# A two-layer LoRA kernel in fp32: W's fourth pair loaded earlier, the images stored by GpSimd, and sums of W's blocks kept one group sooner for two of five products

## The chip, the cores and the metric

One Trainium2 chip, one core. The metric is the device time of the kernel in microseconds, the median of several executions; lower is better.

## What is computed

```python
x = x + (x @ B[id0].T) @ A[id0].T              # layer 0, adapter of rank 16, scaling 1
x = x + x @ W.T + b + 2 * ((x @ A1[id1].T) @ B1[id1])   # layer 1, adapter of rank 16, scaling 2
```

x is 8 x 512 x 2048, W is 2048 x 2048, everything is float32, and each of the 8 batch elements ("units") has its own adapters. Nearly all arithmetic is x @ W.T.

## The kernel before

**The multiplication.** Each number is split into a high part in fp32r and a low part, and a product is made of three matmuls: high by high, low by high, high by low (L530, L531, L532). Two units of x make a group, so there are four groups. Within a group a Strassen-like scheme of seven products over half matrices replaces eight. Five of the seven products (i = 0, 1, 2, 4, 6) need a sum or a difference of two blocks of W; products 3 and 5 need one block only. A product has eight steps (o = 0 to 7), one for each 128 rows of output, so there are 4 x 7 x 8 = 224 steps, numbered s. A step is 24 matmuls of 128 x 512.

**W.** For step s SyncE loads a block into `w_one` (three slots) and, where a sum is wanted, a second block into `w_two` (two slots), `load_w`. VectorE adds the pair in place (L672, `sum_w`), ScalarE makes the high part (L567) and VectorE the low part (L676, `split_w`). In group 0 all sums are made and thrown away; in group 1 they are made again and stored to `w_sums` in device memory (`keep_sum`); groups 2 and 3 load the stored sums. A `w_one` slot whose sum is stored is reloaded only after that store has landed.

**The adapters.** Work in the background is cut into chunks, and `background(s)` says which chunks go between the matmuls of step s: the first after c = 1 of the step's eight columns c, the second after c = 5, the third after c = 6. In group 0, steps 3 to 16, the 32 chunks are rows of W multiplied with layer 0's A (six matmuls each, L482 to L484); they make four "images" of 128 x 512, and chunk 8j + 7 ends image j. Chunks from step 19 on multiply x with the down adapters (four matmuls, L500 and L501). A chunk's raw data comes by SyncE (`bg_raw`, three slots at first), ScalarE makes its high part (L597), VectorE its low part (L703); there are two buffers for the parts, so that the split of chunk z waits until TensorE is through chunk z - 2. Before step 3 TensorE makes `across` from all units' a1 and a0 (L551).

**Images.** TensorE ends image j with a matmul that needs `b1_rows`; VectorE adds it to the `image` tile, where eight rows of a0 per j have been loaded (L804, one step after the image's last chunk and behind the splits for the step after that). SyncE stores the tile to `images` (L406), two steps of its loop later. GpSimd's queue does the loading, in order: eight `b1_rows` transfers for image j once image j - 1 is done on TensorE, a wait for the store of image j - 1, and eight `image` transfers (L448).

**Order of the queues.** Every engine runs its own loop over s, in program order. VectorE in step s does: the adding of step s - 1's result, the low part of W for s + 1, sums and splits of x for the next product at certain o (`X_SUM_AT`, `X_SPLIT_AT`), the sum of W for s + 2, the splits of the chunks of step s + 1, the rest. At o = 7 the last two splits of x for the next product (L698) come at the very end. ScalarE has the same order. SyncE in step s does: `keep_sum(s + 1)`, `load_w(s + 3)`, loads of x, `store(s - 2)`, the raw chunks of step s + 2, the loads of `sums` for s + 2, the store of an image. Ahead of its loop it loads W for steps 0 to 2, the resident halves of x in quarters (`resident`), eight a1 adapters, the mask and the bias; only then comes W for step 3.

Of the kernel before, what the change touches and what calls it, by code (L numbers as in the profile page):

```python
# [36 lines left out]
SUMMED = [0, 1, 2, 4, 6]  # L37
STAGED = [1, 2, 3, 5, 6]
# [3 lines left out]
SUM_GROUPS = 2  # L42
# [5 lines left out]
X_SPLIT_AT = (2, 4, 7, 7)  # L48

# [15 lines left out]
def background(s):  # L65

    if s >= STEPS:
        return []
    g, i, o = where(s)
    if g:  # L70
        places = (0, 2, 4, 5)
        return [IMAGE + 16 * g + 4 * i + places.index(o)] if i < 4 and o in places else []
    if 3 <= s <= 16:
        first = 2 * (s - 3) + max(0, s - 8) // 2
        return list(range(first, first + (3 if s in (9, 11, 13, 15) else 2)))
    if 19 <= s <= 22:
        return [IMAGE + 2 * (s - 19), IMAGE + 2 * (s - 19) + 1]
    return [IMAGE + 8 + s - 24] if 24 <= s <= 31 else []
# [39 lines left out]
def has_sum(s):  # L118

    return 0 <= s < SUM_GROUPS * PER_GROUP and where(s)[1] in SUMMED  # L120


def keeps_sum(s):
    return has_sum(s) and where(s)[0] == SUM_GROUPS - 1
# [33 lines left out]
def build(nc, x, ids0, ids1, a0, a0_down, b0, w, w_rows, bias, a1, b1, mask, w_sums, images, out):  # L158
    with ExitStack() as ctx:
# [127 lines left out]
        def _(sp):  # L287
            def load_w(s):
                g, i, o = where(s)
                one, two = W_BLOCKS[i]  # L290
                if s >= W_ONES:
                    sp.wait_ge(w_ready, s - W_ONES + 1)
                    if keeps_sum(s - W_ONES):
                        sp.wait_ge(w_kept[s % W_ONES], DMA * kept_in_slot(s - W_ONES))
                if g >= SUM_GROUPS and two:
                    made = PER_GROUP * (SUM_GROUPS - 1) + s % PER_GROUP
                    sp.wait_ge(w_kept[made % W_ONES], DMA * kept_in_slot(made))
                    source = w_sums[SUMMED.index(i), o]
                else:
                    source = w[H * one[1] + o][:, H * one[0]:H * (one[0] + 1), :]  # L300
                sp.dma_start(w_one[s % W_ONES][:, :, :], source).then_inc(w_one_loaded[s % W_ONES], DMA)
                if two and g < SUM_GROUPS:
                    k = sums_before(s)
                    if k >= W_TWOS:
                        sp.wait_ge(w_summed, k - W_TWOS + 1)
                    sp.dma_start(w_two[k % W_TWOS][:, :, :], w[H * two[1] + o][:, H * two[0]:H * (two[0] + 1), :])\
                      .then_inc(w_two_loaded[k % W_TWOS], DMA)
# [68 lines left out]
            for r in range(1, CH):  # L376
                load_resident(0, 0, r)
            sp.wait_ge(ids_loaded, 2 * DMA)
            for n in range(NB):
                sp.dma_start(a1_raw[:, n, :, :], adapter(n, a1).rearrange("u p c r -> (u p) c r"))\  # L380
                  .then_inc(a1_loaded, DMA)
            sp.dma_start(mask_sb, mask).then_inc(mask_loaded, DMA)
            sp.dma_start(bias_sb[:, :], bias).then_inc(bias_loaded, DMA)
            for s in range(STEPS):
# [3 lines left out]
                if s + W_ONES < STEPS:  # L388
                    load_w(s + W_ONES)
                if o in X_LOAD_AT and p + 1 < PRODUCTS * GROUPS:  # L390
                    load_x(p + 1, X_LOAD_AT.index(o))
# [11 lines left out]
                if s - 2 in IMAGE_LAST:  # L403
                    j = IMAGE_LAST[s - 2]
                    sp.wait_ge(image_ready, j + 1)
                    sp.dma_start(images[:, T * j:T * (j + 1)], image[:, :]).then_inc(image_stored, DMA)  # L406
# [6 lines left out]
        def _(pool):  # L413
# [24 lines left out]
            def load_rows(j):  # L438
                cols = slice(T * j, T * (j + 1))
                if j:  # L440
                    pool.wait_ge(image_done, j)
                for n in range(NB):
                    pool.dma_start(b1_rows[R * n:R * (n + 1), :], adapter(1, n, b1).rearrange("u r d -> (u r) d")[:, cols])\
                        .then_inc(b1_rows_loaded, DMA)
                if j:
                    pool.wait_ge(image_stored, DMA * j)
                for n in range(NB):
                    pool.dma_start(image[R * n:R * (n + 1), :], adapter(0, n, a0).rearrange("u r d -> (u r) d")[:, cols])\  # L448
                        .then_inc(a0_rows_loaded, DMA)

# [8 lines left out]
            for s in range(STEPS):  # L459
                g, i, o = where(s)  # L460
                if s + 4 in FIRST:
                    load_down(FIRST[s + 4])
                if i + 1 in RANKED and o == 3:
# [3 lines left out]
        def _(pe):  # L467
# [78 lines left out]
            for s in range(3):  # L546
                step(s)
# [5 lines left out]
            for s in range(3, STEPS):  # L553
# [4 lines left out]
        def _(act):  # L558
# [76 lines left out]
            for s in range(STEPS):  # L635
# [4 lines left out]
                if s == 1:  # L640
                    act.wait_ge(a0_loaded, NB * DMA)
                    act.activation(a0_hi[:, :, :, :], a0_raw[:, :, :, :].rearrange("p n c r -> p c n r"), ACT.Copy)\
                       .then_inc(a0_hi_ready, 1)
                    act.wait_ge(a1_loaded, NB * DMA)
                    act.activation(a1_cols.rearrange("p (c n r) -> p c n r", c=C, n=NB),
                                   a1_raw[:, :, :, :].rearrange("p n c r -> p c n r"), ACT.Copy).then_inc(a1_ready, 1)
                if o in X_SPLIT_AT[:2] and p + 1 < PRODUCTS * GROUPS:
                    split_x(p + 1, X_SPLIT_AT.index(o))
# [16 lines left out]
        def _(dve):  # L665
# [106 lines left out]
            for s in range(STEPS):  # L772
# [6 lines left out]
                if p + 1 < PRODUCTS * GROUPS:  # L779
                    if o in X_SUM_AT:  # L780
                        sum_x(p + 1, X_SUM_AT.index(o))
                    if o in X_SPLIT_AT[:2]:
                        split_x(p + 1, X_SPLIT_AT.index(o))
# [12 lines left out]
                if s == 3:  # L796
# [57 lines left out]
```

## Time and profile before

| | |
|---|---|
| median of 3 runs | 1407.84 us (1407.28 to 1408.16) |
| the profiled execution | 1408.91 us, its span 1407.2 us |
| TensorE busy | 98% of the span, granted clock 0.994 on the mean |
| VectorE, ScalarE, GpSimd busy | 70%, 35%, 7% |
| DMA | 329.37 MB, 234 GB/s over the span |

TensorE's matmuls start one after another without a gap for most of the span. So the time is what TensorE must do, plus the places where it waits or runs at half clock, and these lie almost all in the first 200 us and around two borders between groups.

### The profile page before, as it was taken

Reading aid. Unit: us, or ns where it says so; the run is one execution under the profiler, and the core shown is the slowest. Engines: PE = TensorE matmul, PEld = TensorE weight load, DVE = VectorE, ACT = ScalarE, POOL = GpSimd, SP = SyncE. Lnnn points to the kernel's source line nnn. Section 1 sums busy time; section 2 is a strip of 40 time slices with the busy share of each in tenths; the row PEclk is TensorE's granted clock in tenths of the full one; section 3 lists DMA queues with packets and bytes.
Section 4 is the critical chain, followed back from the end, with each engine's and each line's share of the span. In section 5 each row is a group of like instructions: output and inputs, shape, how many; then the busy total and the mean of one; then the engine's idle time right before and its main releaser. Section 6 shows DMA issues by size and latency. Waiting matters only on the chain.

```text
span 1407.2 us, 16162 instructions
## 1 busy us (share of the span) xinstructions
PE 1372.3 (98%) x5992; PEld 1127.3 (80%) x5992; DVE 983.2 (70%) x1031; ACT 485.5 (35%) x491; POOL 91.7 (7%) x190
## 2 busy tenths in 40 slices
PE   6799989999999999999999999999999999999999
PEld 5687868888887888888887888888888888888887
DVE  4888877786768887687766676666655766666662
ACT  3344334333333344233323343333233334332331
POOL 3012310001000000000001000000101000000000
PEclk9899999999999999999999999999999999999999
DMA  9888974797989888599898335556856444457642
GB/s 346 275 296 296 298 237 129 234 309 261 301 279 354 301 299 294 178 332 354 266 353 275 128 120 157 169 189 211 275 199 228 140 138 135 155 171 249 196 153 83
DMA packets 108654, 329.37 MB, mean 234 GB/s; under 512 B 14496, under 2 KB 15648, under 8 KB 108576
## 3 DMA queue, kind: packets, MB, share of 16 engines
q1 hardware_dynamic: 102240, 316.79, 67.0%
q0 software_dynamic: 6336, 11.55, 2.8%
q8 instruction: 48, 0.79, 0.2%
q14 instruction: 30, 0.25, 0.0%
HBM read 272.70 MB, written 55.57 MB: 233 GB/s over the span
## 4 chain that ended last, share of the span: by engine, by line
PE 89%; DVE 3%; DMA 3%; issue 2%; SPq 1%; ACT 1%; POOLq 0%; POOL 0%; DVEq 0%; ACTq 0%
PE acc L530 27%; PE acc L531 27%; PE acc L532 27%; PE acc L514 2%; PE down_ps L500 2%; PE down_ps L501 2%; DMA w_two<-w 1%; PE image_ps L482 1%; PE image_ps L484 1%; PE image_ps L483 1%; DVE w_one L672 1%; DMA w_sums<-w_one 1%; DVE bg_lo L703 1%; DVE w_lo L676 1%; DMA bg_raw<-x 1%
## 5 line engine op out<-in xcount | busy, mean ns | idle before, releaser
L530 PE MATMUL acc<-x_hi,w_hi 128*128 128x512 f32 x1792 | 703.6, 393 | 15.9 <-DVE x_lo L698 11.5
L531 PE MATMUL acc<-x_lo,w_hi 128*128 128x512 f32 x1792 | 700.7, 391 | 0.0
L532 PE MATMUL acc<-x_hi,w_lo 128*128 128x512 f32 x1792 | 700.3, 391 | 0.0
L567 ACT ACTIVATE w_hi<-w_one 128x1024 fp32r<-128x1024 f32 x224 | 237.5, 1060 | 673.7 <-PE acc L532 606.1
L530 PEld LDWEIGHTS acc<-x_hi,w_hi 128*128 128x128 f32 x1792 | 338.3, 189 | 88.7 <-issue 13.5
L531 PEld LDWEIGHTS acc<-x_lo,w_hi 128*128 128x128 f32 x1792 | 338.4, 189 | 71.8 <-issue 1.0
L532 PEld LDWEIGHTS acc<-x_hi,w_lo 128*128 128x128 f32 x1792 | 337.8, 188 | 71.4
L676 DVE TENSOR_TENSOR w_lo<-w_one,w_hi 128x1024 fp32r<-128x1024 f32 x224 | 273.7, 1222 | 104.9 <-ACT w_hi L567 104.9
L698 DVE TENSOR_TENSOR x_lo<-x_stage,x_hi 128x1024 fp32r<-128x1024 f32 x80 | 96.1, 1222 | 45.2 <-ACT x_hi L586 45.1
L586 ACT ACTIVATE x_hi<-x_stage 128x1024 fp32r<-128x1024 f32 x80 | 83.4, 1056 | 115.2 <-DVE x_stage L692 85.2
L741 DVE SCALAR_TENSOR_TENSOR sums<-acc,bias_sb,sums 128x512 f32<-128x512 f32 x128 | 95.7, 747 | 36.2 <-PE acc L514 36.2
L672 DVE TENSOR_TENSOR w_one<-w_one,w_two 128x1024 f32<-128x1024 f32 x80 | 97.5, 1218 | 25.8 <-DMA w_two<-w 25.8
L703 DVE TENSOR_TENSOR bg_lo<-bg_raw,bg_hi 128x1024 fp32r<-128x1024 f32 x64 | 77.5, 1220 | 27.6 <-ACT bg_hi L597 27.4
L597 ACT ACTIVATE bg_hi<-bg_raw 128x1024 fp32r<-128x1024 f32 x64 | 67.1, 1053 | 71.6 <-PE image_ps L484 49.5
L692 DVE TENSOR_TENSOR x_stage<-x_stage,resident 128x1024 f32<-128x1024 f32 x64 | 78.0, 1219 | 1.7 <-DMA x_stage<-x 1.7
L434 POOL DMA_DIRECT2D rank_raw<-images x48 | 23.4, 487 | 836.3 <-issue 836.3
L500 PE MATMUL down_ps<-bg_hi,down 128*128 128x512 f32 x128 | 51.2, 400 | 9.5 <-DVE down L747 6.0
L726 DVE TENSOR_TENSOR sums<-sums,acc 128x512 f32<-128x512 f32 x32 | 22.0, 687 | 44.7 <-PE acc L532 44.7
L514 PE MATMUL acc<-rank_x,rank_w 96*128 96x512 f32 x128 | 51.0, 399 | 0.0
L501 PE MATMUL down_ps<-bg_lo,down 128*128 128x512 f32 x128 | 50.4, 394 | 0.0
L724 DVE TENSOR_TENSOR sums<-sums,acc 128x512 f32<-128x512 f32 x32 | 21.8, 683 | 31.0 <-PE acc L532 31.0
L731 DVE TENSOR_TENSOR sums<-sums,acc 128x512 f32<-128x512 f32 x32 | 21.9, 684 | 26.5 <-PE acc L532 26.5
(53 smaller groups left out, 626.8 us busy)
## 6 DMA issues: line engine op xcount, KB each, us to landing
w_one<-w SPq DMA_DIRECT2D x144, 512.0 KB, 5.5
w_two<-w SPq DMA_DIRECT2D x80, 512.0 KB, 7.3
w_one<-w_sums SPq DMA_DIRECT2D x80, 512.0 KB, 3.3
x_stage<-x SPq DMA_DIRECT2D x64, 512.0 KB, 4.7
out<-sums SPq DMA_DIRECT2D x128, 256.0 KB, 4.5
w_sums<-w_one SPq DMA_DIRECT2D x40, 512.0 KB, 4.9
resident<-x SPq DMA_DIRECT2D x32, 512.0 KB, 7.7
sums<-x SPq DMA_DIRECT2D x64, 256.0 KB, 5.4
```

The costliest lines, as they stand in the source:

```text
L500: pe.matmul(down_ps[:, :], weights, hi[:, u, :], start=(c == 0), stop=False)
L514: pe.matmul(acc[s % BANKS][:, :], rank_w[:, P * o:P * (o + 1)], rank_x[side][:, :], start=False, stop=True, skip_group_check=True).then_in ...
L530: pe.matmul(ps[:, :], w_hi[ws][:, c, :], hi, start=(c == 0), stop=False)
L531: pe.matmul(ps[:, :], w_hi[ws][:, c, :], lo, start=False, stop=False)
L532: mm = pe.matmul(ps[:, :], w_lo[ws][:, c, :], hi, start=False, stop=(c == H - 1))
L567: act.activation(w_hi[s % W_PARTS][:, :, :], w_one[s % W_ONES][:, :, :], ACT.Copy).then_inc(w_hi_ready, 1)
L586: act.activation(x_hi[q % X_PARTS][:, :, :], x_source(p, r), ACT.Copy).then_inc(x_hi_ready, 1)
L672: dve.tensor_tensor(one, one, w_two[k % W_TWOS][:, :, :], W_SIGN[where(s)[1]]).then_inc(w_summed, 1)
L676: dve.tensor_tensor(w_lo[s % W_PARTS][:, :, :], w_one[s % W_ONES][:, :, :], f32(w_hi[s % W_PARTS][:, :, :]), ALU.subtract).then_inc(w_read ...
L698: dve.tensor_tensor(x_lo[q % X_PARTS][:, :, :], x_source(p, r), f32(x_hi[q % X_PARTS][:, :, :]), ALU.subtract).then_inc(x_ready, 1)
L703: dve.tensor_tensor(bg_lo[z % 2][:, :, :], bg_source(z), f32(bg_hi[z % 2][:, :, :]), ALU.subtract)\
L741: dve.scalar_tensor_tensor(out=tile, in0=acc[s % BANKS][:, :], scalar=bias_sb[:, f:f + 1], in1=tile, op0=ALU.add, op1=ALU.add).then_inc(ba ...
```

## The change

Three edits. (1) SyncE's prologue ends after the second quarter of `resident[0]`; W for step 3 goes ahead of the other two quarters and of all adapters, four adapters go into loop step 0 and four into loop step 1, mask and bias into loop step 3. For that `across` is made before step 5, not 3, the chunks run over steps 4 to 16 with new counts, and product 1's first two splits of x come at o = 4 and 5. (2) GpSimd stores the images itself, between its two groups of loads. (3) Products 4 and 6 keep their sums in group 0 and load them in groups 1 to 3; products 0, 1 and 2 keep them in group 1 as before.

```diff
+KEPT_IN = {0: 1, 1: 1, 2: 1, 4: 0, 6: 0}
-SUM_GROUPS = 2
+def split_at(p):
+    return X_SPLIT_AT if p > 1 else (4, 5, 7, 7)
@@ background
-    if 3 <= s <= 16:
-        first = 2 * (s - 3) + max(0, s - 8) // 2
-        return list(range(first, first + (3 if s in (9, 11, 13, 15) else 2)))
+    if 4 <= s <= 16:
+        counts = (2, 2, 2, 3, 2, 3, 2, 3, 2, 3, 3, 2, 3)
+        first = sum(counts[:s - 4])
+        return list(range(first, first + counts[s - 4]))
@@ has_sum, keeps_sum
-    return 0 <= s < SUM_GROUPS * PER_GROUP and where(s)[1] in SUMMED
+    g, i, o = where(s)
+    return s >= 0 and i in SUMMED and g <= KEPT_IN[i]
-    return has_sum(s) and where(s)[0] == SUM_GROUPS - 1
+    return has_sum(s) and where(s)[0] == KEPT_IN[where(s)[1]]
@@ load_w
-                if g >= SUM_GROUPS and two:
-                    made = PER_GROUP * (SUM_GROUPS - 1) + s % PER_GROUP
+                if two and not has_sum(s):
+                    made = PER_GROUP * KEPT_IN[i] + s % PER_GROUP
...
-                if two and g < SUM_GROUPS:
+                if has_sum(s):
@@ sync, prologue and loop
-            for r in range(1, CH):
-                load_resident(0, 0, r)
-            sp.wait_ge(ids_loaded, 2 * DMA)
-            for n in range(NB):
-                sp.dma_start(a1_raw[:, n, :, :], ...)
-            sp.dma_start(mask_sb, mask).then_inc(mask_loaded, DMA)
-            sp.dma_start(bias_sb[:, :], bias).then_inc(bias_loaded, DMA)
+            load_resident(0, 0, 1)
             for s in range(STEPS):
...
                     load_w(s + W_ONES)
+                if s == 0:
+                    for r in (2, 3):
+                        load_resident(0, 0, r)
+                    sp.wait_ge(ids_loaded, 2 * DMA)
+                if s in (0, 1):
+                    for n in range(4 * s, 4 * s + 4):
+                        sp.dma_start(a1_raw[:, n, :, :], ...)
+                if s == 3:
+                    sp.dma_start(mask_sb, mask).then_inc(mask_loaded, DMA)
+                    sp.dma_start(bias_sb[:, :], bias).then_inc(bias_loaded, DMA)
...
-                if s - 2 in IMAGE_LAST:
-                    j = IMAGE_LAST[s - 2]
-                    sp.wait_ge(image_ready, j + 1)
-                    sp.dma_start(images[:, T * j:T * (j + 1)], image[:, :]).then_inc(image_stored, DMA)
@@ gpsimd
                 if j:
+                    keep_image(j - 1)
                     pool.wait_ge(image_stored, DMA * j)
...
+            def keep_image(j):
+                pool.wait_ge(image_ready, j + 1)
+                pool.dma_start(images[:, T * j:T * (j + 1)], image[:, :]).then_inc(image_stored, DMA)
...
+                if s - 1 in IMAGE_LAST and IMAGE_LAST[s - 1] == 3:
+                    keep_image(3)
@@ tensor: across is made before step 5
-            for s in range(3):
+            for s in range(5):
...
-            for s in range(3, STEPS):
+            for s in range(5, STEPS):
@@ scalar: a1_cols in step 2, behind the high part of W for step 3
+                if s == 2:
                     act.wait_ge(a1_loaded, NB * DMA)
@@ scalar and vector
-                if o in X_SPLIT_AT[:2] and p + 1 < PRODUCTS * GROUPS:
-                    split_x(p + 1, X_SPLIT_AT.index(o))
+                if o in split_at(p + 1)[:2] and p + 1 < PRODUCTS * GROUPS:
+                    split_x(p + 1, split_at(p + 1).index(o))
@@ vector: across is masked in step 5
-                if s == 3:
+                if s == 5:
```

## Rows read from the trace of the kernel before

**Rows 1.** TensorE's waits, whole span: total us, times, longest.
```profile
PE acc L530 <- DVE x_lo L698: 11.5, 1, 11.5
PE down_ps L500 <- DVE down L747: 6.0, 1, 6.0
PE image_ps L482 <- DVE bg_lo L703: 5.0, 2, 4.0
PE acc L530 <- DVE w_lo L676: 4.4, 2, 3.7
PE down_ps L500 <- DVE bg_lo L703: 2.5, 3, 1.4
...
PE down_ps L500 <- issue: 1.1, 1, 1.1
```

**Rows 2.** Timeline of TensorE: `across`, then step 16: start, duration, and the idle time before.
```profile
32.36 3.81 PE L551 MATMUL down_ps<-a_raw,sums 128*128 128x128 f32 x32 [1.16 <-ACT sums L645]
...
162.87 0.39 PE L530 MATMUL acc<-x_hi,w_hi 128*128 128x512 f32 x1
...
165.59 0.39 PE L530 MATMUL acc<-x_hi,w_hi 128*128 128x512 f32 x1
```

**Rows 3.** Windows of TensorE: stretch, length, busy (matmuls), granted clock, DMA share, GB/s.
```profile
45.70:51.60 5.90, 5.90 (x14) 0.50 0.87 262
...
191.20:195.00 3.80, 3.80 (x9) 0.51 0.89 306
```

**Rows 4.** Timeline of SyncE's queue, 0 to 45 us.
```profile
11.25 10.65 SPq L380 DMA_DIRECT2D a_raw<-a  x8
...
24.42 0.43 SPq L306 DMA_DIRECT2D w_two<-w  x1
```

**Rows 5.** Timeline of VectorE, 30 to 40 us.
```profile
34.10 1.22 DVE L672 TENSOR_TENSOR w_one<-w_one,w_two 128x1024 f32<-128x1024 f32 x1 [8.73 <-DMA w_two<-w]
35.24 2.28 DVE L792 TENSOR_TENSOR a_lo<-a_raw,a_hi 128x2048 fp32r<-128x2048 f32 x1
```

**Rows 6.** Timeline of ScalarE, 27 us.
```profile
27.13 1.93 ACT L642 ACTIVATE a_hi<-a_raw 128x2048 fp32r<-128x2048 f32 x1 [3.02 <-DMA a_raw<-a_down]
```

**Rows 7.** DMA view: all transfers from 0 to 26 us, and from 0 to 38 us.
```profile
DMA packets 2931, 9.08 MB, mean 349 GB/s; under 512 B 449, under 2 KB 633, under 8 KB 2931
...
DMA packets 5307, 13.13 MB, mean 346 GB/s; under 512 B 959, under 2 KB 2111, under 8 KB 5304
```

**Rows 8.** The chain that ended last, 159 to 181 us: start, us, what.
```profile
159.28 5.12 DMA images<-image
...
173.54 6.41 DMA image<-a
```

**Rows 9.** Timeline of VectorE, steps 15 to 18.
```profile
164.90 2.35 DVE L698 TENSOR_TENSOR x_lo<-x_stage,x_hi 128x1024 fp32r<-128x1024 f32 x2
...
180.05 0.69 DVE L804 TENSOR_TENSOR image<-image_ps,image 128x512 f32<-128x512 f32 x1 [4.41 <-DMA image<-a]
...
181.73 0.63 DVE L724 TENSOR_TENSOR sums<-sums,acc 128x512 f32<-128x512 f32 x1
...
190.63 0.41 DVE L747 SCALAR_TENSOR_TENSOR down<-down_raw,down 128x256 fp32r<-128x256 f32 x1
```

**Rows 10.** Windows of all engines; the last two columns are DMA share and GB/s.
```profile
416.00:455.00 39.00, 37.59 (x164) 30.20 (x164) 32.66 (x36) 11.68 (x11) 3.98 (x8) 1.00 1.01 352
616.00:660.00 44.00, 44.00 (x193) 35.82 (x192) 34.92 (x38) 13.01 (x13) 2.88 (x6) 1.00 1.00 366
```

**Rows 11.** SyncE's queue: the first chunk's load ahead of groups 1 and 2.
```profile
403.75 0.43 SPq L340 DMA_DIRECT2D bg_raw<-x  x1
...
739.21 0.48 SPq L340 DMA_DIRECT2D bg_raw<-x  x1
```

**Rows 12.** Timeline of TensorE: the first matmuls of steps 56 and 112.
```profile
416.04 0.39 PE L530 MATMUL acc<-x_hi,w_hi 128*128 128x512 f32 x1
...
747.61 0.39 PE L530 MATMUL acc<-x_hi,w_hi 128*128 128x512 f32 x1
```

More of the change, by code:

```diff
@@ L375, in _ @@
             load_sum(1)
-            for r in range(1, CH):
-                load_resident(0, 0, r)
-            sp.wait_ge(ids_loaded, 2 * DMA)
-            for n in range(NB):
-                sp.dma_start(a1_raw[:, n, :, :], adapter(n, a1).rearrange("u p c r -> (u p) c r"))\
-                  .then_inc(a1_loaded, DMA)
-            sp.dma_start(mask_sb, mask).then_inc(mask_loaded, DMA)
-            sp.dma_start(bias_sb[:, :], bias).then_inc(bias_loaded, DMA)
+            load_resident(0, 0, 1)
             for s in range(STEPS):
@@ L389, in _ @@
                     load_w(s + W_ONES)
+                if s == 0:
[4 more added lines that the diff above has]
+                    for n in range(4 * s, 4 * s + 4):
+                        sp.dma_start(a1_raw[:, n, :, :], adapter(n, a1).rearrange("u p c r -> (u p) c r"))\
+                          .then_inc(a1_loaded, DMA)
+                if s == 3:
+                    sp.dma_start(mask_sb, mask).then_inc(mask_loaded, DMA)
+                    sp.dma_start(bias_sb[:, :], bias).then_inc(bias_loaded, DMA)
                 if o in X_LOAD_AT and p + 1 < PRODUCTS * GROUPS:
@@ L781, in _ @@
                         sum_x(p + 1, X_SUM_AT.index(o))
-                    if o in X_SPLIT_AT[:2]:
-                        split_x(p + 1, X_SPLIT_AT.index(o))
+                    if o in split_at(p + 1)[:2]:
+                        split_x(p + 1, split_at(p + 1).index(o))
                 if s - 1 in LAST:
```

## The prediction

> **What bounds the kernel now.** I read the page first: TensorE is busy for 98% of the span, so only two things can give time, less work on TensorE or fewer of its gaps. The change takes no matmul away. So I listed TensorE's waits over the whole span [rows 1] and asked of each whether the change touches it. The reader is to see that they are few: 11.5 us at the start, then 1.2 us [rows 2] and 3.7 us ahead of step 3, 4.0 us at the first chunk, 0.7 + 6.0 us in step 19, 1.0 us in step 13, 2.5 us in three waits of group 1 and 1.1 us at step 112. Undisturbed, twelve matmuls take 165.59 - 162.87 = 2.72 us [rows 2], or 0.227 us each; a plain step of 24 takes 5.44 us, a chunk of six 1.36 us. Then windows over the stretches behind the two longest waits [rows 3]: after the wait of 4.0 us fourteen matmuls ran at 0.50 of the clock, after that of 6.0 us nine, at 0.2 us lost for each: 2.8 and 1.8 us. Behind the waits of 3.7 and 1.4 us no such stretch follows. Last the timelines of the other engines around each wait, to find what was late.
>
> **The early load of W.** Before, step 3 of TensorE waits for this: SyncE issues eight a1 adapters, which hold its queue for 10.7 us, and sends the second block of W for step 3 only at 24.42 [rows 4]; it lands at 34.1, 8.7 us after VectorE stands ready for it [rows 5]. The DMA engines are saturated: 9.08 MB have moved by 26 us, 13.13 MB by 38 us [rows 7], which is 0.3375 MB per us. So a transfer lands when the bytes issued ahead of it are through, and I count bytes. In the new order that block goes out at about 16.5 us (it waits for the sum of step 1), with 9.4 MB in all to land up to and including it: the loads of W for steps 0 to 3 (4.2 MB), six quarters of x (3.1), two `sums` (0.5), GpSimd's a0 (1.0), and some 0.5 of later things that move beside them. That gives 26 + (9.4 - 9.08) / 0.3375 = 27.0 us, 7 us sooner. TensorE can't use all of it. ScalarE makes a0_hi from 27.13 [rows 6], VectorE's a_lo follows at 29.1, and in this trace step 3 begins 4.7 us after a_lo begins (from 35.24 to 32.36 + 3.81 + 3.7 = 39.9, where the wait behind `across` ends [rows 1, 2]). So step 3 starts at 33.8; step 2 ends at 32.36 - 1.2 = 31.2 [rows 2]; wait 2.6 us, say 2.7 with the edge of the last matmul. W for step 4 lands when 12.5 MB are through (one more W pair, two quarters of x, four adapters, a `sums` and GpSimd's rows), at 36.1. The a1 adapters issued in loop step 1 land near 38; ScalarE's conversion of them (1.9 us, as that of a0 [rows 6]) stands ahead of its part of W for step 4, which takes 1.1 us more and VectorE's low part 1.2: step 4 starts at 42.4, step 3 ended at 33.8 + 5.4 = 39.2; wait 3.1 us. The first chunk's raw data is behind 15.1 MB, 43.8 us; with both splits TensorE has it at 46.1, where it asks at 43.8; wait 2.3 us. Sum after: 8.1 us of waits in three pieces, each below the 3.7 us behind which no slow stretch followed. Sum before: 1.2 + 3.7 + 4.0 + 2.8 of clock = 11.7. **Gain 3.6 us.** `across` itself (3.8 us) is only moved, as are the two chunks of step 3. Bounds: if the clock falls after all, 0.8 us; if each transfer lands 1 us sooner than counted, 6.6 us; if a1 lands 3 us later, the wait ahead of step 4 is 6 us with a slow stretch, and 2 us are lost.
>
> The Trainium skill (TensorE: Matmul & The Clock Gate, HAM oscillation) says that it is a long unbroken idle stretch of TensorE that lets its clock fall to 1.2 GHz, each time anew. The trace agrees as far as it goes: 0.50 is that level of 2.4 GHz, seen behind 4.0 and 6.0 us. By that rule three short waits cost their own length alone; by a count of idle time alone, 2.8 us would go again.
>
> **The images on GpSimd's queue.** Before, VectorE stands still until 180.05 for a0 rows of image 3 [rows 9], because the store of image 2 went out at 159.28 and took 5.1 us, then eight loads, the last of which landed 6.4 us after 173.54 [rows 8]. Its step 18 therefore starts at 181.73 and ends with the down adapter at 190.63 + 0.41 [rows 9], where TensorE resumes at 191.2. In the new order GpSimd waits for image j itself. Image 2's last chunk is the third of step 13 as before, and VectorE adds it behind the splits for step 15, near 158 us on this time scale; the store lands at about 163.5, a0 is there by 179. But the last image's step 16 now ends later (below), so that VectorE asks at 179: no wait, to 1.5 us either way. What is late next is step 18 of VectorE by its own length. It can start only when step 17's matmuls end, which is when TensorE starts step 18. It needs what stands between 181.73 and 191.2, that is 9.5 us, and I add 0.8 us for ScalarE's high part of W, which was long ready before and will now be made in that time: 10.3 us. TensorE asks for the chunk after step 18 and two columns of step 19, 5.44 + 1.36 = 6.8 us. So 3.5 us of wait stay. Before: 0.7 + 6.0 + 1.8 of clock + 0.4 at half clock around them = 8.9; after: 3.5 + 0.3. **Gain 5.1 us.** If 3.5 us is enough for the clock to fall, 3.3.
>
> The move brings little else. SyncE loses three waits that nothing was late behind. The Trainium skill (DMA: Bandwidth & Descriptors, Issuing engines are not separate DMA queues) speaks against a quicker store: it says transfers of all issuers run on the same 16 engines and only issue time is saved. The sum counts none.
>
> **The chunks' new places.** Step 16 now has three chunks, and it is the first step of a product. The third chunk's high part waits until the first (c = 1) is multiplied, for there are two buffers; behind it, in ScalarE's and VectorE's program order, stand the last two splits of x for this very product, which TensorE wants at c = 4. Before, step 16 had two, and VectorE was through both at 162.63 + 2.27 = 164.90, where x_lo begins [rows 9], 2.1 us ahead of need. After: from the last matmul of the c = 1 chunk, 0.3 us to ScalarE, 1.1 for its part, 1.15 for bg_lo, 1.25 for x_lo (two take 2.35 [rows 9]), together 3.8 us, against seven matmuls, 1.6 us. **Loss 2.2 us and 0.3 around it.** Two steps with three chunks in a row (13 and 14) leave VectorE 0.2 us late for step 15: **loss 0.2.** Bounds: nothing, if the third chunk's split goes quicker than any row shows, and 5 us, if its raw data is late too.
>
> **The sums kept sooner.** In group 1 products 4 and 6 drop 16 second blocks, 16 stores and 16 additions; TensorE waited for none of them but at step 112, so this gives 1.1 + 0.3 = **1.4 us**. In exchange group 0 stores 16 sums. For product 4 this is group 1's product 4 over again, which runs at 366 GB/s without a wait [rows 10]: nothing. Product 6 stands directly ahead of group 1's product 0, which already takes 352 GB/s with the DMA engines always busy [rows 10] and shows the largest wait of 1.4 us. The load of the first chunk leads step 56 by 416.04 - 403.75 = 12.3 us; at step 112, behind a product 6 that stores, the lead is 747.61 - 739.21 = 8.4 us [rows 11, 12] and TensorE waits 1.1. So product 6 with stores leaves SyncE 3.9 us more behind, and product 0 at full load has no room to catch up. **Loss 3.9 us**, in step 56 and the chunk steps 58 to 61. Net **2.5 us lost**. Bounds by bytes: the sixteen steps move 33.6 MB in 92.8 us of matmuls; at 366 GB/s they take 91.8, the loss is 0 and the net a gain of 1.4; at 320 GB/s, a tenth below the 352, they take 105, of which 2.2 us of today's waits are to be taken off: 10 lost, 8.6 net.
>
> **Sum.** -3.6 - 5.1 + 2.5 + 0.2 + 2.5 = -3.5 us on the profiled execution, 1408.9 - 3.5 = 1405.4. It ran 1.1 us above the median of 1407.8, so the median should be 1404.4.
>
> **Rivals.**
> *The borders cost nothing (23%).* Product 0 keeps up as group 1's product 4 did at 366 GB/s, and the net is -1.4: 1404.4 - 3.9 = 1400.5; with x's splits in time at step 16 as well, 1398. For it: no wait in group 1's product 4. Against it: 352 with a wait.
> *The early part gives nothing (18%).* The order only swaps transfers within a saturated queue; the a1 conversion in ScalarE's way makes one long wait ahead of step 4, and the clock falls. Then 3.6 is gone: about 1408. Against it: 7 us of lead for W's pair.
> *Slower: stores of sums starve the border (13%).* Place: steps 56 to 63. If these sixteen steps get 320 GB/s, the net loss there is 8.6 instead of 2.5, 1410.5. It decides from a net loss of 8.8 us on, against the 0.2% bound. For it: a store holds its `w_one` slot until it lands, so that saturation delays SyncE's whole queue, chunks included. Against it: 366 GB/s has been reached.
> *As forecast (46%)*: 1404.4, by itself 1401.5 to 1407.
>
> **The numbers.** 0.2%, or 2.8 us, is about what this measurement can tell from no change: the bound lies at 1405.0. Of the forecast's 46%, 29 lie below it, 16 within, 1 above; of the first rival 23 below; of the second 1 below, 14 within, 3 above; the third lies above but for 2. Faster 53%, same 32%, slower 15%. The range 1398.5 to 1410 leaves out the far ends of the first and third rival.
>
> **What would show it.** Right: the wait ahead of step 3 below 3 us, a second one ahead of step 4, none of 4 us before 50 us and no window at 0.50 there; no idle of VectorE on a0 rows at image 3, but still 3 to 4 us of TensorE on the down adapter in step 19; a new wait on x_lo in step 16; waits on bg_lo at steps 56 to 61 above 4 us together, none at 112. Wrong: step 19 without any wait, a slow stretch in the first 60 us, or a border as it was.

## The result and the profile after

Median 1411.01 us (18 runs, 1408.6 to 1413.7) against 1407.88 us of the kernel before in the same rounds: ratio 1.0019, 95% interval 1.0012 to 1.0027. The change made the kernel 3.1 us slower, just inside the 0.2%. The forecast was 1404.4 us, with a range from 1398.5 to 1410.

The profiled execution took 1409.31 us, 1.7 us less than the median, with a span of 1407.5 us. Busy times hardly move, except that VectorE makes 16 additions fewer:

```profile
PE 1373.3 (98%) x5992; PEld 1128.7 (80%) x5992; DVE 967.0 (69%) x1015; ACT 484.7 (34%) x491; POOL 94.1 (7%) x194
```

TensorE's waits over the whole span, to be laid beside [rows 1]. L546, L498, L516 and L715 are the old L530, L482, L500 and L698:

```profile
PE acc L546 <- DVE x_lo L715: 13.6, 2, 11.4
PE acc L546 <- DVE w_lo L693: 5.3, 4, 2.7
PE down_ps L516 <- DVE down L764: 3.6, 1, 3.6
PE down_ps L516 <- issue: 3.4, 1, 3.4
PE image_ps L498 <- DVE bg_lo L720: 3.3, 2, 1.9
PE down_ps L516 <- DVE bg_lo L720: 1.7, 3, 0.6
```

The 11.4 us stand at the start, as before. Nothing is left of a wait of 4 us, step 19's is 3.6 instead of 0.7 + 6.0, and ahead of step 3 it is 2.7 instead of 1.2 + 3.7. New are 1.3 us ahead of step 4, 2.2 us on x_lo (13.6 - 11.4) in step 16 and 3.4 us at step 56. The list is close to the forecast one. What it doesn't show is in the windows (stretch, length, busy, granted clock, DMA share, GB/s), where [rows 3] had two slow stretches and this has four:

```profile
33.90:42.50 8.60, 7.34 (x24) 0.80 1.06 331
```
```profile
164.40:169.00 4.60, 4.57 (x13) 0.63 0.51 150
...
188.50:192.00 3.50, 3.46 (x9) 0.54 1.00 342
```
```profile
418.00:424.60 6.60, 6.57 (x17) 0.56 1.03 397
```

TensorE had run matmuls without a gap for at least 5 us before each of these waits. Behind them its granted clock is down from the full level, 2.4 GHz, to the half one, 1.2 GHz, for a part of each stretch. Thirteen matmuls take 2.95 us at full clock, not 4.6; seventeen take 3.85, not 6.6. A slow stretch now stands behind waits of 2.7, 2.2, 3.6 and 3.4 us.

Where the time went can be read off the starts of the same step in both traces. The last column takes off 0.227 us for each background matmul (chunks, ranks and images) that one kernel has done more by then; `across` has its own length, 3.81 us.

| step begins | before | after | after minus before, for the same work |
|---|---|---|---|
| 9 | 97.24 | 91.55 | -4.3 |
| 13 | 133.51 | 127.87 | -4.3 |
| 16 | 162.87 | 157.95 | -3.6 |
| 17 | 171.92 | 172.47 | +0.55 |
| 19 | 183.63 | 183.38 | -0.25 |
| 20 | 198.92 | 196.02 | -2.9 |
| 56 | 416.04 | 413.12 | -2.9 |
| 57 | 422.64 | 426.06 | +3.4 |
| 62 | 454.76 | 456.84 | +2.1 |
| 113 | 755.57 | 755.89 | +0.3 |

So 4.3 us are won early; 4.8 are lost by step 17, mostly in step 16; 3.4 come back in steps 18 and 19; 6.3 are lost in step 56 and 1.3 of them come back by step 62; 1.8 come back by step 113, 1.4 of them at step 112 and 0.4 in group 1's product 4 (steps 88 to 95), which now loads its sums.

In this trace the early part went as counted. SyncE's queue sent the second block of W for step 3 at 16.35, and VectorE had it at 26.3, 7.8 us sooner than in [rows 5] (both timelines: start, duration, and the wait ahead of it):

```profile
16.35 0.33 SPq L315 DMA_DIRECT2D w_two<-w  x1
```
```profile
26.34 1.22 DVE L689 TENSOR_TENSOR w_one<-w_one,w_two 128x1024 f32<-128x1024 f32 x1 [0.91 <-DMA w_two<-w]
...
41.15 1.22 DVE L693 TENSOR_TENSOR w_lo<-w_one,w_hi 128x1024 fp32r<-128x1024 f32 x1 [2.72 <-ACT w_hi L583]
...
163.17 2.35 DVE L715 TENSOR_TENSOR x_lo<-x_stage,x_hi 128x1024 fp32r<-128x1024 f32 x2
...
177.39 0.69 DVE L821 TENSOR_TENSOR image<-image_ps,image 128x512 f32<-128x512 f32 x1 [1.20 <-DMA image<-a]
...
187.97 0.42 DVE L764 SCALAR_TENSOR_TENSOR down<-down_raw,down 128x256 fp32r<-128x256 f32 x1
```

Here are also the three other places. W's low part for step 4 waits 2.7 us for ScalarE, whose high part had to wait for the conversion of the a1 adapters. Step 16's x_lo begins at 163.17, 5.2 us into the step, not 2.0 us as in [rows 9]. And image 3 still waits 1.2 us for its rows. The chain that ended last says why, to be laid beside [rows 8]:

```profile
152.99 7.14 DMA images<-image
...
169.78 7.51 DMA image<-a
```

The store of image 2 takes 7.1 us here, where it took 5.1 before, and the last of the rows behind it 7.5, not 6.4. The first of the eight loads of rows goes out 8.3 us behind the store's issue. The experiments show below that the longer time isn't GpSimd's doing.

At step 56 it is the first chunk's raw data that comes late: SyncE sends its load at 405.33, and ScalarE stands ready for it 5.2 us before it lands (SyncE's queue and ScalarE's timeline):

```profile
405.33 0.44 SPq L349 DMA_DIRECT2D bg_raw<-x  x1
```
```profile
414.29 1.06 ACT L613 ACTIVATE bg_hi<-bg_raw 128x1024 fp32r<-128x1024 f32 x1 [5.17 <-DMA bg_raw<-x]
```

In the eight steps ahead, group 0's product 6 now moves 353 GB/s with a DMA share of 0.98; before it was 293 GB/s and 0.90.

### The profile page after: what moved, and what is told of

Same layout as the page of the kernel before. It is cut to its first block, busy times and chain, and to the rows that moved or that the text cites. A ratio compares the mean times of both kernels' runs of the same rounds, so it can differ in the third digit from the quotient of the medians.

```text
span 1407.5 us, 16133 instructions
## 1 busy us (share of the span) xinstructions
PE 1373.3 (98%) x5992; PEld 1128.7 (80%) x5992; DVE 967.0 (69%) x1015; ACT 484.7 (34%) x491; POOL 94.1 (7%) x194
## 4 chain that ended last, share of the span: by engine, by line
PE 86%; DMA 6%; DVE 4%; issue 2%; SPq 1%; ACT 1%; POOLq 0%; POOL 0%; DVEq 0%; ACTq 0%
PE acc L546 26%; PE acc L547 26%; PE acc L548 26%; PE down_ps L516 2%; PE acc L530 2%; PE down_ps L517 2%; DMA bg_raw<-w_rows 1%; DMA w_two<-w 1%; DVE bg_lo L720 1%; DMA w_sums<-w_one 1%; DVE w_one L689 1%; DVE w_lo L693 1%; DMA bg_raw<-x 1%; PE image_ps L498 1%; DMA image<-a 1%
## 5 line engine op out<-in xcount | busy, mean ns | idle before, releaser
L546 PE MATMUL acc<-x_hi,w_hi 128*128 128x512 f32 x1792 | 704.5, 393 | 18.9 <-DVE x_lo L715 13.6
L546 PEld LDWEIGHTS acc<-x_hi,w_hi 128*128 128x128 f32 x1792 | 338.6, 189 | 92.8 <-issue 14.0
L715 DVE TENSOR_TENSOR x_lo<-x_stage,x_hi 128x1024 fp32r<-128x1024 f32 x80 | 96.1, 1222 | 43.0 <-ACT x_hi L602 42.8
L689 DVE TENSOR_TENSOR w_one<-w_one,w_two 128x1024 f32<-128x1024 f32 x64 | 78.0, 1219 | 23.3 <-DMA w_two<-w 23.2
L516 PE MATMUL down_ps<-bg_hi,down 128*128 128x512 f32 x128 | 51.5, 403 | 8.7 <-DVE down L764 3.6
L530 PE MATMUL acc<-rank_x,rank_w 96*128 96x512 f32 x128 | 51.1, 399 | 0.0
```

The costliest lines, as they stand in the source:

```text
L516: pe.matmul(down_ps[:, :], weights, hi[:, u, :], start=(c == 0), stop=False)
L530: pe.matmul(acc[s % BANKS][:, :], rank_w[:, P * o:P * (o + 1)], rank_x[side][:, :], start=False, stop=True, skip_group_check=True).then_in ...
L546: pe.matmul(ps[:, :], w_hi[ws][:, c, :], hi, start=(c == 0), stop=False)
L689: dve.tensor_tensor(one, one, w_two[k % W_TWOS][:, :, :], W_SIGN[where(s)[1]]).then_inc(w_summed, 1)
L715: dve.tensor_tensor(x_lo[q % X_PARTS][:, :, :], x_source(p, r), f32(x_hi[q % X_PARTS][:, :, :]), ALU.subtract).then_inc(x_ready, 1)
```

## The experiments

Each was timed in five rounds, beside runs of the kernel before. All ratios are to that kernel; the changed kernel's is 1.0019 or, measured again, 1.0020. The rows come from three sets of rounds, in which the kernel before had medians of 1408.8, 1408.1 and 1408.8 us, so kernels of different sets are compared by their ratios.

| kernel | median us | ratio, 95% interval |
|---|---|---|
| changed kernel again | 1411.68 | 1.0020 (1.0011 to 1.0029) |
| two chunks in step 16 | 1410.20 | 1.0011 (1.0001 to 1.0022) |
| all sums kept in group 1 | 1407.75 | 0.9988 (0.9977 to 0.9999) |
| SyncE stores the images | 1418.04 | 1.0063 (1.0050 to 1.0077) |
| both of the first two | 1406.58 | 0.9989 (0.9980 to 0.9998) |
| both, ScalarE stores | 1406.35 | 0.9990 (0.9979 to 1.0000) |
| the same, product 4 kept in group 0 | 1407.39 | 1.0000 (0.9991 to 1.0009) |
| edit 1 alone | 1411.93 | 1.0037 (1.0024 to 1.0051) |
| edit 2 alone | 1407.99 | 0.9996 (0.9985 to 1.0008) |
| changed kernel, waits filled | 1408.26 | 1.0002 (0.9991 to 1.0012) |
| down adapters one step later | 1401.86 | 0.9959 (0.9946 to 0.9972) |
| the same, waits filled | 1400.45 | 0.9950 (0.9936 to 0.9963) |

**The changed kernel once more.** No edit.

> The changed kernel itself once more, beside the others on the same chip. Theory A': its executions differ by whether the clock falls behind waits near 2 to 3 us; another profile shows the same waits to 0.3 us but other slow stretches, and the time is 1409 to 1413. Rival E: waits themselves differ from execution to execution by more than 1 us, by the order in which transfers land.

Its profiled execution took 1409.54 us. The waits:

```profile
PE acc L546 <- DVE x_lo L715: 13.6, 2, 11.3
PE down_ps L516 <- DVE down L764: 5.7, 1, 5.7
PE image_ps L498 <- DVE bg_lo L720: 4.8, 2, 2.6
PE acc L546 <- DVE w_lo L693: 4.5, 4, 2.8
PE down_ps L516 <- issue: 2.3, 1, 2.3
```

And the windows behind three of them, in steps 16, 19 and 56:

```profile
165.40:169.50 4.10, 4.07 (x18) 1.00 0.53 160
190.00:195.00 5.00, 4.96 (x12) 0.50 0.90 308
419.50:424.00 4.50, 4.49 (x13) 0.64 1.03 394
```

Both theories hold a part. The wait in step 16 is the same 2.25 us as before, yet here nothing is slow behind it, while in the first trace thirteen matmuls ran at 0.63. So one and the same wait may cost its length or nearly 2 us more. Two other kernels below have this wait too, of 2.25 us each: behind it the granted clock is 0.64 where all sums are kept in group 1 (166.2 to 171.0 us) and 1.00 where SyncE stores the images (171.2 to 175.0 us). And the wait in step 19 is 5.7 us, not 3.6: VectorE waited 3.3 us for image 3's rows instead of 1.2. So waits that hang on a transfer differed by 2 us between these two executions. Both profiled executions are among the fastest of the changed kernel.

**Two chunks in step 16.**

```diff
-        counts = (2, 2, 2, 3, 2, 3, 2, 3, 2, 3, 3, 2, 3)
+        counts = (2, 2, 3, 3, 2, 3, 2, 3, 2, 3, 2, 3, 2)
```

> The changed kernel with the chunk counts of steps 4 to 16 as 2, 2, 3, 3, 2, 3, 2, 3, 2, 3, 2, 3, 2, so that step 16 has two chunks again and steps 9 to 16 are as in the kernel before. Theory A (the third chunk of step 16 holds up the last two splits of x, and the wait lets the clock fall): the 2.2 us wait on x_lo in step 16 and the slow stretch behind it go, work-adjusted loss between steps 16 and 17 falls from 4.1 us to below 0.5, and the time falls by 3 to 4.5 us against the changed kernel, to about 1407. Rival B (VectorE has a fixed amount to do before step 19, so the loss only moves there, with image 3 now late): step 16 clean but step 19's wait grows from 3.6 us by 2 or more, time within 1.5 us of the changed kernel.

Waits, and VectorE at the image:

```profile
PE acc L546 <- DVE x_lo L715: 11.4, 1, 11.4
PE down_ps L516 <- DVE down L764: 5.9, 1, 5.9
```
```profile
156.90 0.68 DVE L821 TENSOR_TENSOR image<-image_ps,image 128x512 f32<-128x512 f32 x1
178.18 0.69 DVE L821 TENSOR_TENSOR image<-image_ps,image 128x512 f32<-128x512 f32 x1 [4.21 <-DMA image<-a]
```

The wait on x_lo in step 16 is gone, so the third chunk was its cause. But rival B came closer: TensorE reaches step 17 earlier while the rows of image 3 come when they come, and VectorE waits 4.2 us for them. Step 19 takes back most of what step 16 gives; by the ratios 1.3 us remain, with intervals that overlap.

**All sums kept in group 1.**

```diff
-KEPT_IN = {0: 1, 1: 1, 2: 1, 4: 0, 6: 0}
+KEPT_IN = {0: 1, 1: 1, 2: 1, 4: 1, 6: 1}
```

> The changed kernel with all sums of W kept in group 1, as before. Theory A (stores in product 6 of group 0 put SyncE's queue behind at step 56): the wait of 3.4 us at step 56 and its slow stretch go (6.3 us), step 61's wait goes back to 1.4 us (+0.8) and step 112's 1.4 us comes back: net gain about 4 us against the changed kernel, to about 1407. Rival C (the border is slow because of what the early edits changed upstream, not because of the stores): the wait at step 56 stays at 2 us or more, no change.

```profile
PE down_ps L516 <- DVE bg_lo L720: 2.8, 4, 1.5
...
PE down_ps L516 <- issue: 1.3, 1, 1.3
```

Step 56 runs without a wait, step 61's is back at 1.5 and step 112's at 1.3 us. 0.32% of 1408 us is 4.5 us: theory A to half a microsecond. This is the largest loss that undoing one edit takes away. Edit 3 was only taken off, never put on alone.

**SyncE stores the images.** The changed kernel with edit 2 undone.

> The changed kernel with the images stored by SyncE again, two loop steps behind. Theory A (GpSimd's stores spare VectorE the wait for image 3's rows of a0, and SyncE's lateness was what delayed them): VectorE waits 3 us or more for image 3, step 19's wait grows from 3.6 us to 5 or 6, and the time rises by 1.5 to 4 us. Rival D (the store goes out at the same time either way, since image 2 is added late): within 1 us of the changed kernel.

VectorE's images, SyncE's store of image 0, and TensorE's waits on chunks:

```profile
98.35 0.68 DVE L822 TENSOR_TENSOR image<-image_ps,image 128x512 f32<-128x512 f32 x1
127.06 0.69 DVE L822 TENSOR_TENSOR image<-image_ps,image 128x512 f32<-128x512 f32 x1 [3.68 <-DMA image<-a]
```
```profile
105.16 0.43 SPq L419 DMA_DIRECT2D images<-image  x1
```
```profile
PE image_ps L499 <- DVE bg_lo L721: 6.4, 2, 4.0
```

6.4 us slower than with GpSimd's stores, more than either theory said. It is image 1 that hurts, not image 3: its rows come late because image 0 is stored at 105.2, VectorE waits 3.7 us at 127, and step 13 has 4.0 us of wait with slow matmuls behind it. In the new order image 0 ends a step later than before (VectorE adds it at 98.35 instead of 90.22), while image 1 is asked for sooner (at 123.4 instead of 127.17), and SyncE's 6.8 us between adding and storing now count.

**Edit 1 alone**, and **edit 2 alone.**

> Edit 1 alone: the early load of W's fourth pair with its new order, images stored by SyncE, all sums kept in group 1, chunk counts of steps 9 to 16 as in the kernel before. Theory A (the early edit alone gives its 3.6 to 4.3 us, and shifts everything by that): 1404 to 1405 and step 13 and 19 as before. Rival I (the gain is given back, since the images, which SyncE stores two steps late, are then later against TensorE): VectorE waits for images 1 and 3, step 13's wait grows from 1.0 to 4 us, and the time is 1407 or more.

> Edit 2 alone: the kernel before, with GpSimd storing the images. Theory A (SyncE's late stores of images 0 and 1 are what makes the rest of the image chain late): image 1 and 2 are stored 8 us or more earlier, VectorE's wait for image 3 shrinks, step 19's wait falls from 6.0 by 1 to 2.5 us, 1 to 3 us faster than before. Rival N (image 3's rows hang on the store of image 2, which goes out at the same time either way and takes longer from GpSimd): VectorE's wait for image 3 stays 4 us or more, no change.

Edit 1 alone: step 17 begins 3.6 us later than before for the same work, though step 13 still begins 1.25 us earlier. TensorE's waits on chunks:

```profile
PE image_ps L499 <- DVE bg_lo L721: 7.0, 3, 4.1
```

Edit 2 alone, VectorE's last image, and GpSimd's stores of images 0 and 1:

```profile
179.87 0.69 DVE L807 TENSOR_TENSOR image<-image_ps,image 128x512 f32<-128x512 f32 x1 [4.32 <-DMA image<-a]
```
```profile
91.24 0.59 POOL L450 DMA_DIRECT2D images<-image  x1 [1.69 <-DVE image L807]
128.06 0.58 POOL L450 DMA_DIRECT2D images<-image  x1 [8.01 <-DVE image L807]
```

The stores of images 0 and 1 go out 8 and 9 us earlier than SyncE's (99.3 and 137.5), and it brings nothing, for image 2 is added at 158.5 either way: rivals I and N. Edit 1 needs edit 2: alone it gives 1.0037, with edit 2 and two chunks in step 16 it gives 0.9989 (next). Edit 2 without edit 1 has nothing to do.

**Both undone, then ScalarE as the issuer.** The second kernel stores right behind ScalarE's high part of W:

```diff
+                if s - 2 in IMAGE_LAST:
+                    j = IMAGE_LAST[s - 2]
+                    act.wait_ge(image_ready, j + 1)
+                    act.dma_start(images[:, T * j:T * (j + 1)], image[:, :]).then_inc(image_stored, DMA)
```

> The changed kernel with both undone: two chunks in step 16 (counts as in the first experiment) and all sums kept in group 1. Theory A (costs of steps 16 and 56 add up): 1.0 us of the first and 3.5 us of the second off the changed kernel, about 1407, with step 19's wait near 6 us. Rival B (what step 16 gives always comes back in step 19): the same 1407.7 as with the sums alone undone, within 1 us.

> As the kernel with both undone, but ScalarE issues the store of an image, right behind its high part of W in the step after the one that ends the image, in place of GpSimd. Theory F (a store issued by GpSimd takes 7 us against 5 to 6 by another queue, and that keeps image 3's rows of a0 late): VectorE's wait for image 3 shrinks from 4 us by 2 us or more, step 19's wait from 5.9 to 3.5 or 4, time about 2 us lower than with GpSimd. Rival G (the rows themselves, eight loads one after another, are the long part, and DMA is busy): VectorE still waits 3 us, no change in time.

The first undoing adds nothing to the second by the ratios (0.9989 and 0.9988), so rival B holds again. With ScalarE image 3 is added at 177.35, 20.8 us behind image 2, against 21.7 with GpSimd; VectorE still waits 3.7 us, and step 19 has 5.9 us. Theory F falls, and its premise too, for the traces have the store of image 2 from all three issuers (us from issue to landing):

| kernel | chunks in step 16 | issuer | store of image 2 |
|---|---|---|---|
| before; edit 1 alone | two | SyncE | 5.1; 5.3 |
| two chunks in step 16; edit 2 alone; both undone | two | GpSimd | 3.8; 4.0; 4.3 |
| ScalarE stores; product 4 kept in group 0; late down adapters, plain and filled | two | ScalarE | 4.1; 4.4; 4.5; 3.3 |
| changed kernel, twice; sums in group 1; waits filled | three | GpSimd | 7.1; 8.1; 7.2; 7.4 |
| SyncE stores the images | three | SyncE | 8.7 |

The store is slow where step 16 has three chunks and quick where it has two, whoever issues it. The new chunk counts of steps 14 to 16, not the queue, go with the longer store; by what way isn't shown.

**Product 4 kept in group 0, product 6 in group 1.**

> As the kernel whose images ScalarE stores, with product 4's sums kept in group 0 and product 6's in group 1. Theory A (only product 6, which stands right ahead of group 1, hurts at the border): no wait above 0.5 us at step 56, time within 1 us of that kernel. Rival H (any extra stores in group 0 put the queue behind): a wait at step 56 or in product 4 of 1 us or more, time 2 us higher.

```profile
PE down_ps L509 <- DVE bg_lo L717: 2.5, 3, 1.4
PE down_ps L509 <- issue: 1.1, 1, 1.1
```

The 1.1 us is at step 112, and step 56 has no wait. The profiled execution loses nothing in product 4 of group 0, and gains 0.4 us in steps 88 to 95; the median is 1.0 us above the kernel with none kept there, with overlapping intervals. So it was product 6 that hurt, and keeping product 4's sums early costs nothing that can be told and gives nothing in the median either.

**Filling the waits.** `fill` multiplies parts of x that are at hand into the free PSUM bank; nobody reads it.

```diff
+            def fill(s, count):
+                for _ in range(count):
+                    held = x_hi[CH * (s // H) % X_PARTS]
+                    pe.matmul(idle_ps[:, :], held[:, 0, 0:P], held[:, 0, :], start=True, stop=True)
...
+                    if c == 4:
+                        fill(s, {16: 8}.get(s, 0))
...
+                    if c == 1:
+                        fill(s, {19: 14, 56: 10}.get(s, 0))
```

> The changed kernel, with matmuls whose result nobody reads put where TensorE waits anyway: 8 in step 16 ahead of c = 4, 14 in step 19 and 10 in step 56 ahead of the first chunk, into the one free PSUM bank. They take 1.8, 3.2 and 2.3 us at full clock, about the waits or less. Theory J (the waits cost more than their length because the clock falls behind them): the waits end at the same moments, the slow stretches of 1 to 3 us behind each go, and the time falls by 3 to 6 us against the changed kernel, to 1405 to 1408. Rival K (the slow matmuls are not due to idleness, or would come anyway): no gain, or a loss of up to 2 us where the filling outlasts a wait.

TensorE's timeline at the three places, and the windows behind them:

```profile
164.07 1.98 PE L537 MATMUL idle_ps<-x_hi 128*128 128x512 f32 x8
166.48 0.50 PE L556 MATMUL acc<-x_hi,w_hi 128*128 128x512 f32 x1 [0.43 <-DVE x_lo L727]
```
```profile
185.24 3.33 PE L537 MATMUL idle_ps<-x_hi 128*128 128x512 f32 x14
190.78 0.47 PE L517 MATMUL down_ps<-bg_hi,down 128*128 128x512 f32 x1 [2.21 <-DVE down L776]
```
```profile
415.25 2.43 PE L537 MATMUL idle_ps<-x_hi 128*128 128x512 f32 x10
418.33 0.47 PE L517 MATMUL down_ps<-bg_hi,down 128*128 128x512 f32 x1 [0.66 <-issue]
```
```profile
166.50:171.00 4.50, 4.50 (x20) 1.00 0.57 152
190.80:195.00 4.20, 4.20 (x19) 1.00 1.02 310
418.30:423.00 4.70, 4.67 (x20) 1.00 1.03 409
```

32 matmuls more, and the kernel is faster: 1.0002 against 1.0020, that is 2.5 us, with intervals that just touch. All three stretches behind the filled waits run at full clock. In the same trace two waits that were not filled, 2.4 us ahead of step 3 and 3.4 us ahead of step 4, were followed by a granted clock of 1.00 (33.7 to 42.7 us) and of 0.54 (42.7 to 50.0 us). The mean granted clock of an execution tells the same without a trace: 0.996 to 0.999 in all twelve of the filled kernel, 0.992 to 0.995 in all 29 of the changed kernel. So filling keeps the clock up, which is theory J's mechanism; its amount of 3 to 6 us was too high. Filling and rest of the wait last 2.4, 5.5 and 3.1 us together, and step 19's 5.5 stand against 3.6 in the first trace. Against that trace, and for the same work, 1.5 us are saved in step 16, nothing in steps 18 and 19, and 3.1 in step 56: what is saved ahead of step 19 VectorE's queue takes back there.

**The down adapters one step later.** On the kernel with product 4 kept in group 0 and ScalarE's stores:

```diff
-    if 19 <= s <= 22:
-        return [IMAGE + 2 * (s - 19), IMAGE + 2 * (s - 19) + 1]
+    if 20 <= s <= 22:
+        return [[IMAGE, IMAGE + 1], [IMAGE + 2, IMAGE + 3, IMAGE + 4], [IMAGE + 5, IMAGE + 6, IMAGE + 7]][s - 20]
```

> As the kernel with product 4's sums kept in group 0, product 6's in group 1 and the images stored by ScalarE, but the first unit's eight chunks of the down adapters in steps 20 to 22 (2, 3, 3) instead of 19 to 22 (2 each). Theory L (VectorE's own length between step 17's end and the first chunk is what holds TensorE in step 19, on top of image 3's late rows): one step more of time, the waits of 0.9 + 6.0 us shrink to 2 to 3.5 together and the slow stretch goes: 4 to 5 us faster, about 1402.5. Rival M (the chunks crowded into steps 21 and 22 hold VectorE up there, or the wait only moves): within 1.5 us.

```profile
PE down_ps L509 <- DVE down L761: 2.5, 1, 2.5
```
```profile
188.00:196.00 8.00, 5.55 (x24) 1.00 1.02 288
```

VectorE still waits 2.6 us for the rows, yet TensorE's wait on the down adapter is 2.5 us instead of 6.0 and no matmul behind it is slow (those of step 4 are: 0.55 of the clock from 42.4 to 50.0 us). By the ratios this is 0.41%, or 5.8 us, faster than the kernel it was made from and than the kernel before: theory L, and somewhat more than its 4 to 5 us. With the waits filled as well:

> As the one with the late down adapters, with filling matmuls at steps 3 and 4 ahead of the first matmul (8 each), ahead of the first chunk in steps 4 (6), 13 (3) and 20 (4). Theory J: the slow stretch in step 3 or 4 (0 to 2 us, it differs by execution) never comes, and the spread of the times shrinks: 1 to 2 us faster than without filling. Rival K: no gain.

Filling in steps 3, 4, 13 and 20 gives 1.4 us of median, within overlapping intervals, so theory J's gain isn't shown here, nor is a smaller spread (4.0 us between the fastest and slowest of six, 4.5 without filling). The clock does rise: 0.999 or 1.0 in all six executions, against 0.996 to 0.998 without filling. This has the lowest median: 0.9950 (0.9936 to 0.9963).

## Why the prediction was wrong

**The step that failed** is the one that priced short waits at their length. For the early load it stood as "8.1 us of waits in three pieces, each below the 3.7 us behind which no slow stretch followed", and it was used again for step 16 ("2.2 us and 0.3 around it"), for step 19 ("3.5 + 0.3") and, without a word, for step 56. One wait of 3.7 us without a slow stretch had been read as a bound, and that reading was wrong. In the trace before, step 3 resumes at 39.91, behind the wait of 3.7 us, and only six matmuls run until the wait of 4.0 us begins. The windows of TensorE over them and over that wait show that the clock fell at 41.3, before the second wait had begun:

```profile
39.90:41.30 1.40, 1.39 (x6) 1.00 1.03 331
41.30:45.60 4.30, 0.37 (x2) 0.50 1.02 340
```

So the fourteen slow matmuls of [rows 3] ran at a clock that had fallen 1.4 us behind the end of the 3.7 us wait, and the trace gave no ground to call waits below 3.7 us free. A fallen clock was priced only as an edge of the range, at 2.8 us for the early load and 1.8 for step 19, and not at all for steps 16 and 56. The runs show slow stretches behind 2.7, 2.2, 3.4 and 3.6 us, and none behind 2.25 in another execution. In the profiled execution these stretches, with the edges of the waits, cost about 1.9 us in step 3 (of no effect, since W's low part for step 4 was later still), 1.9 in step 16, 1.7 in step 19 and 3.0 in step 56. Filling three of the waits gave 2.5 us back. The change took a few long waits and made them more and shorter ones. By the forecast that saves the clock. In fact the mean granted clock stayed at 0.992 to 0.995, as before: the places where it can fall have become more.

The same step holds for the early load, where the two traces of the changed kernel hide it. Eleven traces have edit 1 and no filling in steps 3 and 4. In three of them, both of the changed kernel among these, the clock is at 1.00 from 46 to 50 us, and in the other eight at 0.50 to 0.67. For the same work step 5 begins 3.6 to 4.3 us sooner than before in the three and 2.0 to 2.9 in the eight; the median of all is 2.7.

The Trainium skill (TensorE: Matmul & The Clock Gate, HAM oscillation) names long unbroken idle stretches as what lets the clock fall, and the prediction took from it that short waits cost their own length alone. The traces differ: they show falls behind waits of 2.2 and 2.7 us too, and the measurement decides.

**Point by point:**

- *Early load, -3.6.* Right in place, and in these two traces in size: -4.3 in the first, -4.1 in the second (start of step 13). That the size came out is in part luck, as the other traces show. W for step 3 was there at 26.3 (27.0 forecast), step 3 began at 33.9 (33.8), step 4 at 42.5 (42.4), the first chunk at 46.1 (46.1). Alone it turned into a loss of 0.37%, because SyncE's stores then make image 1 late. That this edit hangs on edit 2 was not foreseen. One of the prediction's signs of being wrong, a slow stretch in the first 60 us, did come: 0.80 of the clock from 33.9 to 42.5 us.
- *Images, -5.1.* 3.4 us came back in steps 18 and 19; the slow stretch behind the wait took 1.7. The wait that remains was 3.6 us (3.5 forecast) in the first trace and 5.7 in the second. Image 3's rows were 1.2 us late in the first, inside the 1.5 us that the prediction allowed, and 3.3 in the second, outside it. The 3.5 has luck in it: the 0.8 us for ScalarE's high part of W did not show (it ran from 178.20 to 179.26, while VectorE was still at image 3 and the clearing of `down` behind it), and VectorE instead began step 18's work 1.1 us behind TensorE (179.07 against 177.94). The Trainium skill (DMA: Bandwidth & Descriptors, Issuing engines are not separate DMA queues) was cited against a quicker store from GpSimd. The traces agree: the store of image 2 took 3.8 to 8.1 us from GpSimd, 5.1 to 8.7 from SyncE and 3.3 to 4.5 from ScalarE in the kernels of the table above.
- *Step 16, +2.2.* The wait was 2.24 us, its cause the third chunk. With the slow stretch it came to 4.1, and 0.7 went in steps 13 to 15, where 0.2 was forecast. That undoing it brings only 1.3 us or nothing, since step 19 takes the rest, was not foreseen: these two terms are not independent.
- *Border, +3.9 and -1.4.* 5.0 lost by step 62 and 1.8 back by step 113. The lead of the first chunk's load shrank from 12.3 to 413.12 - 405.33 = 7.8 us; 3.4 of wait came from that, the rest from the clock. The wait came all in step 56, not spread over 56 to 61; step 61's even fell to 0.6.
- *Sum.* The terms as measured in the profiled execution give -4.3 + 4.8 - 3.4 + 3.2 = +0.3 instead of -3.6 + 2.7 - 5.1 + 2.5 = -3.5. The miss of 3.8 us is 2.1 at steps 13 to 16, 1.7 at the images and 0.7 at the border, less 0.7 at the early load. The medians differ by 3.1, so the forecast missed the median by 6.6. The remaining 2.8 us lie in which execution was profiled: before 1.0 us above its median, after 1.7 below. For the second trace the latter is 2.1. The forecast carried the first of these distances over to the changed kernel. No trace shows one of its slower executions; that they are those with a slow stretch in step 4 is likely from the eleven traces above, and would be worth about 1.5 us, but it isn't shown. Over its 29 executions the median is 1410.0 us where the mean granted clock is 0.995 and 1412.1 where it is 0.993 or less.
- *The rival "stores of sums starve the border"* had the place right and the mechanism too, a queue that falls behind. Its size of 8.6 us net did not come; one late chunk and the clock behind it made 3.2.

Left open is why one wait of 2.25 us is followed by slow matmuls in two of four traces. Length alone doesn't tell: with product 4 kept in group 0 TensorE waited 3.5 us for the first chunk, until 46.7, and the clock stayed at 1.00.

## What to carry to other kernels

A wait of TensorE costs its length and, at the 2 to 6 us seen here, may cost 1.5 to 3 us more in slow matmuls; price it with both ends, and where a wait can't be removed, fill it with matmuls whose result nobody reads. Before calling a wait free, read the granted clock from its start to the start of the next one, for the fall can come when matmuls run again. One or two traces can show the lucky case: compare the same place in every trace at hand. When a stall is removed, work out the length of the next engine's queue between the same two events: here VectorE's nine microseconds of work between step 17 and the first down adapter (179.07 to 188.39) were the real limit, and moving the consumer one step later brought more than all three edits. Try edits of a schedule one by one and together: of three here one was harmful without another, one was idle alone, and undoing the third gave 4.5 us at a border that already ran on full DMA.

## What was not expected of the hardware

- The same wait of 2.24 or 2.25 us in step 16 was followed by thirteen matmuls at 0.63 of the clock in one execution and by eighteen at 1.00 in another.
- In the kernel before, the clock fell 1.4 us after TensorE had resumed behind a wait of 3.7 us, six matmuls on; in steps 16 and 19 of the changed kernel it fell as the wait ended, and at step 56 at 417.1, 0.9 us before the end.
- Filling three waits with 32 matmuls lifted the mean granted clock of the changed kernel's executions from at most 0.995 to at least 0.996.
- The store of a 128 x 512 tile took 3.3 to 8.7 us at one and the same place of the schedule. It did not go by the issuing engine: GpSimd's took 3.8 us in one kernel and 8.1 us in another.
